# Moving the scatter of two of 36 groups of edge attributes out of the time before graph layer 1, into it

## The chip, the core and the metric

The kernel runs on one core of a Trainium2 chip. The metric is the device time of one launch in microseconds (us). The core has TensorE (matmuls, PE in the profile, PEld for its weight loads), VectorE (DVE), ScalarE (ACT), GpSimd (Pool, POOL in the profile) and SyncE (SP), which here issues DMAs only. Each runs its own program in order; semaphores order them among each other. DMAs are issued by SP, ScalarE and Pool and carried out by 16 DMA engines.

## The reference, cut to what matters

6250 nodes with 128 features, 200000 edges sorted by destination, each with an attribute row of 128 numbers.

```python
# 1. one attention layer on layer-normalised x, added to x
# 2. three graph layers on h = relu(layernorm(x)):
for i in range(3):
    msg = relu(x[src] + edge_attr)                 # 200000 x 128
    aggr = segment_sum(msg, dst, num_segments=6250)
    h = x + aggr
    h = relu(bn(h @ W1[i] + b1[i]))                # bn over all nodes
    x = bn(h @ W2[i] + b2[i])                      # relu after it but for the last
```

All of it is float32. `edge_attr` (102 MB) is read in each of the three layers.

## The kernel before, in words

**Edges and slots.** The edges are cut into 52 and a part groups of 3840 (128 partitions x T = 30 columns). The first 36 groups (`BUCKETS`) are handled in graph layers by source block: there are 49 blocks of 128 source nodes, and each edge of a group gets a slot (rank in its block, block). A table in DRAM, `attr_by_slot` (`attr_table` in the code), has for each group 128 x 49 rows of 128 numbers; an edge's attributes lie at its slot. It is cleared, and then filled by *scatters*: SP loads half a group (15 columns) of attributes into one of two places of `abuf` (`load_half`, L608), and Pool issues an indirect DMA for each column t, which writes 128 rows of 512 bytes to the slots that `ridx[:, g, t]` names (`scatter_half`, L797; the DMA has L808). That makes 36 x 30 = 1080 scatters. The other edges (from 36 x 3840 on) are handled in 69 *units* of 7 x 128 edges, by a gather of the source's row for each column.

**Stages.** Edges are sorted into slots (to about 690 us), with the first 15 half groups scattered beside it. Then comes attention, a loop over 49 blocks x 9 chunks, in which TensorE never rests; Pool scatters the other half groups beside it. A scatter waits at every second column until TensorE's chunks have come to a given point (`s_added`, `PACE`). After attention the rows are normalised and turned, SP stores the node rows and the rows that layer 1 gathers (`gin_rows`), and layer 1 begins. Before its first group VectorE (L1556) and SP (L736) each wait until all scatters have landed; VectorE's wait stands ahead of `rest(0, 0)` (L1566), on which ScalarE's `second_part` (L1050) and, behind it in ScalarE's program, the copies of turned columns (L1030) depend, and with those TensorE's last transposes.

**A graph layer** goes over the 36 groups. A group is 7 chunks of 7 blocks, cut into 14 half steps h (4 and 3 blocks in turn). In each, ScalarE puts attributes into a bank (`seed`, L1074), TensorE adds the source rows by matmuls with one-hot matrices (`gather`, L1910), ScalarE and VectorE take the relu (L1082, L1592), and TensorE adds up by destination (`sum_half`, L1928 and L1931). Once a group, at h = 3, TensorE turns the sum of the group before (L1942). In layer 1 VectorE also makes the one-hot matrix of sources for each chunk (`turn_sources`, L1578), from a row that SP has loaded (L703); SP stores the matrix for the later layers (L698) and loads the attributes of the chunk from the table (L712).

Two units belong to a group, k = 0 and 1. For one, SP loads attributes (`load_unit`, L726), Pool gathers seven times (L853), VectorE adds the two at h = 3 or 10 (`add_unit`, L1612), ScalarE takes the relu (L1094), TensorE sums at h = 6 or 11 (L1952). Pool's program in a layer is a plain row, written out for all 36 groups:

```python
for i in range(BUCKETS):
    for k in [...units of group i...]:
        pool.wait_ge(s_uraw, ...)                  # the unit two before this has been added
        for t in range(tiles_of(i, k)):
            pool.wait_ge(s_used, ... 14 * i + 7 * k + t - GATHER_LEAD)   # half steps summed
            pool.indirect_dma_start(out=unit_x[...], ...)                # L853
```

The gathers may so run up to 10 half steps ahead of the sums. SP's program is a loop over groups, in which the loads of a group are issued beside the work on the group before (`load_group`, L728).

Of the kernel before, what the change touches and what calls it, by code (L numbers as in the profile page):

```python
# [5 lines left out]
ALU = mybir.AluOpType  # L6
ACT = mybir.ActivationFunctionType
AX = mybir.AxisListType
F32 = mybir.dt.float32
# [131 lines left out]
SORT_LOADS = 13  # L141
CLEAR_LOADS = 14
# [15 lines left out]
assert (2 * BUCKETS - SORT_LOADS) * HALF_T // PACE - PACE_AHEAD <= BLOCKS * A_CHUNKS  # L158
# [3 lines left out]
def build(nc, x, src, dst, edge_attr, edge_weight, W, a, W1, b1, g_mlp, be_mlp, W2, b2, g_out, be_out, out):  # L162
    ctx = ExitStack()
    with ctx:
# [101 lines left out]
        row_part = ridx[:, :, :].bitcast(F32)  # L266

# [69 lines left out]
        gsm, at = placed("gsm", [P, 2, STEP], F32, at)  # L337

# [99 lines left out]
        loads = [(g, h * HALF_T, HALF_T) for g in range(BUCKETS) for h in range(2)]  # L438

        def scattered(k):  # L440

            return 16 * sum(n for _, _, n in loads[k % 2:k + 1:2])

# [81 lines left out]
        def _(sp):  # L525
# [202 lines left out]
            def load_group(n, i):  # L728
                before = i - 1 if n == 0 else None
                for h in range(G_HALVES):  # L730
                    if h % 2 == 0:
                        load_chunk(n, i, h // 2, before)
                    if h % BY_UNIT == LOAD_AT and unit_at(i, h) is not None:
                        load_unit(n, i, unit_at(i, h))

# [4 lines left out]
            for n in range(LAYERS):  # L740
                load_group(n, 1)
                with sp.Fori(2, BUCKETS - 1) as i:
                    load_group(n, i)
                load_group(n, BUCKETS - 1)
# [14 lines left out]
        def _(pool):  # L759
# [51 lines left out]

            def listed(t, g, most):
                return pool.value_load(t[0:1, g], min_val=0, max_val=most)
# [21 lines left out]
            for n in range(LAYERS):  # L835
# [8 lines left out]
                for i in range(BUCKETS):  # L844
                    for k in [unit_at(i, h) for h in range(0, G_HALVES, BY_UNIT) if unit_at(i, h) is not None]:
# [3 lines left out]
                        for t in range(tiles_of(i, k)):  # L849

                            half = G_HALVES * i + BY_UNIT * k + t - GATHER_LEAD
                            pool.wait_ge(s_used, G_HALVES * (n * BUCKETS + 1) + half)
                            pool.indirect_dma_start(out=unit_x[:, half_place(k), t, :], out_offset=None, in_=gin_rows[n],  # L853
                                                    in_offset=bass.IndirectOffsetOnAxis(ap=unit_src[:, u, t:t + 1], axis=0)).then_inc(s_ug[half_place(k)], 16)

# [311 lines left out]
        def _(vec):  # L1167
# [148 lines left out]
            def place_rows(g):  # L1316
# [7 lines left out]
                link(vec.scalar_tensor_tensor(ridx[:, g, :], rank[:, g, :], float(BLOCKS), row_part[:, g, :], ALU.mult, ALU.add))  # L1324
                vec.copy_predicated(ridx[:, g, :], left_over[:, g, :].bitcast(I32), trash_row[:, :]).then_inc(s_ridx, 1)
# [704 lines left out]
```

## Time and profile before

| | |
|---|---|
| time, median of 3 runs | 4406.07 us (4400.14 to 4413.49) |
| the profiled execution | 4423.43 us, its span 4421.7 us |
| busy share of the span | PE 89%, DVE 81%, ACT 70%, POOL 70% |
| sorting and first scatters | to about 690 us |
| attention | about 690 to 1832 us |
| layer 1, first to last turn of a group's sum (L1942) | 1974.69 to 2752.09 us |
| scatters (L808) | 1080, 1342.9 us busy |
| gathers of units (L853) | 1449, 1671.4 us busy |

The table is read so: Pool's two kinds of indirect DMA fill (1342.9 + 1671.4) of the 3075.0 us that Pool is busy. The busy time of such a DMA is the time in which Pool makes it, not that in which data moves. The page's shares are averages over stages with different limits, so the rows further down are each of one stretch.

### The profile page before, as it was taken

The numbers are of one execution on the slowest core, as the hardware profiler recorded it, in microseconds if no ns is written. First come the engines' busy times: TensorE is split into PE (matmuls) and PEld (weight loads), VectorE is DVE, ScalarE is ACT, GpSimd is POOL, SyncE is SP. The second block draws the span as 40 slices with busy tenths as digits, with TensorE's granted clock in tenths as the row PEclk, the third lists the DMA queues.
The fourth block names the chain that finished last, engine by engine and source line by source line (L and its number), as shares of the span: only waits on it lengthen the run. The fifth ranks groups of instructions, "written<-read, shape, count | busy, mean of one in ns | idle before, by whom it ended". The sixth has DMA issues, their size and how long they took to land.

```text
span 4421.7 us, 151084 instructions
## 1 busy us (share of the span) xinstructions
PE 3951.3 (89%) x50487; PEld 3786.6 (86%) x50488; DVE 3592.8 (81%) x6829; ACT 3095.0 (70%) x7892; POOL 3075.0 (70%) x2584
## 2 busy tenths in 40 slices
PE   4899966999999999649999999699999979999998
PEld 3899966999999999639999998588898858888896
DVE  7899964777777777538888898699899968899897
ACT  3899954777777777536666676677777767777776
POOL 0388874777777777748787786377777727777773
PEclk7888878999999999869999999799999989999999
DMA  9988878998989889569999998488888838888885
GB/s 141 236 291 269 265 274 263 242 257 244 251 248 252 248 244 254 163 208 328 332 346 328 333 341 291 149 290 295 273 292 288 283 115 273 273 289 293 285 290 171
DMA packets 701344, 1161.55 MB, mean 263 GB/s; under 512 B 155914, under 2 KB 525916, under 8 KB 700908
## 3 DMA queue, kind: packets, MB, share of 16 engines
q1 hardware_dynamic: 486780, 816.61, 55.4%
q10 hardware_dynamic: 133200, 176.14, 16.4%
q0 software_dynamic: 81184, 166.43, 11.3%
q8 instruction: 110, 1.80, 0.2%
q14 instruction: 70, 0.57, 0.0%
HBM read 912.73 MB, written 246.56 MB: 262 GB/s over the span
## 4 chain that ended last, share of the span: by engine, by line
POOL 31%; PE 28%; issue 15%; DVE 11%; DMA 5%; SPq 4%; ACT 3%; DVEq 2%; ACTq 0%; POOLq 0%; PEld 0%; PEldq 0%
POOL attr_by_slot L808 29%; PE ps L1910 10%; PE ps L1928 7%; PE ps L1952 5%; PE ps L1931 3%; DVE dst_hot L1585 3%; DMA unit_x<-gin_rows,unit_src 2%; DVE unit_attr L1612 2%; DVE all_split_msg L1592 2%; POOL unit_x L853 2%; DMA abuf<-in_edge_attr 1%; ACT all_split_msg L1082 1%; PE ps L2003 1%; DVE unit_hot L1608 1%; DVEq L1596 1%
## 5 line engine op out<-in xcount | busy, mean ns | idle before, releaser
L853 POOL DMA_INDIRECT unit_x<-gin_rows,unit_src x1449 | 1671.4, 1153 | 496.2 <-issue 382.0
L808 POOL DMA_INDIRECT attr_by_slot<-abuf,ridx x1080 | 1342.9, 1243 | 505.4 <-issue 327.1
L1910 PE MATMUL ps<-x_parts,src_turned 128*128 128x128 bf16 x15876 | 1153.3, 223 | 99.5 <-ACT ps L1074 69.9
L1910 PEld LDWEIGHTS ps<-x_parts,src_turned 128*128 128x128 fp8e4 x15876 | 955.4, 100 | 164.9 <-issue 122.5
L975 ACT ACTIVATE val<-ps,val 128x128 f32<-128x128 f32 x2597 | 720.0, 376 | 182.9 <-DVE val L1433 182.9
L1074 ACT ACTIVATE ps<-sums 128x512 f32<-128x512 f32 x1512 | 834.9, 552 | 6.0 <-DVE all_split_msg L1592 3.6
L1585 DVE TENSOR_TENSOR dst_hot<-iota_one,dl_slot 128x896 fp32r<-128x896 f32 x756 | 819.9, 1085 | 0.7 <-PE ps L1928 0.7
L1928 PE MATMUL ps<-all_split_msg,dst_hot 128*128 128x256 f32 x3528 | 660.8, 308 | 56.1 <-DVE all_split_msg L1592 47.6
L1592 DVE SCALAR_TENSOR_TENSOR all_split_msg<-ps,all_split_msg 128x512 fp32r<-128x512 f32 x1008 | 607.9, 621 | 110.4 <-ACT all_split_msg L1082 95.3
L1837 PE MATMUL ps<-val,src_hot 128*128 128x129 f32 x5194 | 693.8, 283 | 0.8 <-DVE sums L1373 0.3
L1082 ACT ACTIVATE all_split_msg<-ps 128x512 fp32r<-128x512 f32 x1008 | 546.7, 543 | 143.9 <-PE ps L1910 141.5
L1824 PE MATMUL ps<-h_win,turned_hot 128*128 128x130 bf16 x7791 | 585.6, 221 | 44.3 <-issue 19.8
L1837 PEld LDWEIGHTS ps<-val,src_hot 128*128 128x128 f32 x5194 | 619.7, 192 | 1.3 <-DVE sums L1373 0.5
L1928 PEld LDWEIGHTS ps<-all_split_msg,dst_hot 128*128 128x128 f32 x3528 | 488.6, 194 | 80.0 <-issue 64.3
L1824 PEld LDWEIGHTS ps<-h_win,turned_hot 128*128 128x128 bf16 x7791 | 503.8, 97 | 50.9 <-issue 38.3
L1094 ACT ACTIVATE unit_attr<-unit_attr 128x896 f32<-128x896 f32 x207 | 196.9, 951 | 375.0 <-DVE unit_attr L1612 373.0
L1826 PE MATMUL ps<-s_parts,turned_hot 128*128 (+1 forms) x2597 | 433.2, 167 | 0.0
L1425 DVE TENSOR_TENSOR src_hot<-iota_one,low 128x768 f32<-128x768 f32 (+1 forms) x441 | 415.7, 943 | 0.0
L1952 PE MATMUL ps<-unit_hot,unit_attr 128*128 128x64 f32 x2898 | 355.1, 275 | 16.5 <-ACT unit_attr L1094 16.5
L1952 PEld LDWEIGHTS ps<-unit_hot,unit_attr 128*128 128x128 f32 x2898 | 349.2, 196 | 17.7 <-ACT unit_attr L1094 17.3
L1421 DVE TENSOR_REDUCE z<-ps 128x6 f32<-128x24 f32 (+1 forms) x490 | 83.5, 179 | 272.8 <-PE ps L1826 271.9
L1612 DVE TENSOR_TENSOR unit_attr<-unit_attr,unit_x 128x896 f32<-128x896 f32 x207 | 225.5, 1090 | 76.5 <-DMA unit_x<-gin_rows,unit_src 76.2
(255 smaller groups left out, 5816.2 us busy)
## 6 DMA issues: line engine op xcount, KB each, us to landing
sums<-attr_by_slot SPq DMA_DIRECT2D x756, 448.0 KB
turned_hot<-rows_by_block ACTq DMA_DIRECT2D x392, 384.0 KB
attr_by_slot<-zeros SPq DMA_DIRECT2D x36, 3136.0 KB
unit_attr<-in_edge_attr SPq DMA_DIRECT2D x204, 448.0 KB
abuf<-in_edge_attr SPq DMA_DIRECT2D x72, 960.0 KB
src_row<-rows_by_group SPq DMA_DIRECT2D x252, 224.0 KB
src_turned<-src_hots SPq DMA_DIRECT2D x504, 112.0 KB
src_hots<-src_turned SPq DMA_DIRECT2D x252, 112.0 KB
```

What stands on the lines that cost most here:

```text
L808: pool.indirect_dma_start(out=attr_table, out_offset=bass.IndirectOffsetOnAxis(ap=ridx[:, g, t0 + t:t0 + t + 1], axis=0), in_=abuf[:, k % ...
L853: pool.indirect_dma_start(out=unit_x[:, half_place(k), t, :], out_offset=None, in_=gin_rows[n], in_offset=bass.IndirectOffsetOnAxis(ap=uni ...
L975: ins = act.activation(val[:, slot, t, 0:D], given(slot, t)[:, 0:D], ACT.Copy, scale=val[:, slot, t, D:SUM])
L1074: act.activation(ps[:, BANK[h], 0:tiles * D].rearrange("p (b d) -> p b d", d=D), attr[:, first:first + tiles, :], ACT.Copy).then_inc(s_see ...
L1082: act.activation(to, ps[:, BANK[h], 0:tiles * D].rearrange("p (b d) -> p b d", d=D), ACT.Relu).then_inc(s_msg, 1)
L1585: vec.tensor_tensor(dst_hot[:, HOT[c], :, :], iota_one[:, :].unsqueeze(1).to_broadcast([P, G_TILES, P]), dl.rearrange("p o b -> p (o b)"). ...
L1592: vec.scalar_tensor_tensor(split_msgs[n][:, SPLIT_PLACES[n][c], 1, inner, :], ps[:, BANK[h], 0:tiles * D].rearrange("p (b d) -> p b d", d= ...
L1824: pe.matmul(to[:, 0:ROW], turned_hot[:, 0, at:at + P], window_of(g)[:, part * ROW:(part + 1) * ROW], start=(t % 3 == 0 and part == 0), sto ...
L1837: ins = pe.matmul(ps[:, 6, 0:SUM], src_hot[:, slot, t, :], val[:, slot, t, :], start=(c == 0 and t == 0), stop=(c == A_CHUNKS - 1 and t == ...
L1910: ins = pe.matmul(ps[:, BANK[h], k * D:(k + 1) * D], src_turned[:, b * P:(b + 1) * P], x_parts[:, part, b, :], start=False, stop=(k == til ...
L1928: ins = pe.matmul(ps[:, 7, 0:2 * D].rearrange("p (k d) -> p k d", d=D), dst_hot[:, HOT[c], b % G_TILES, :], split_msgs[n][:, SPLIT_PLACES[ ...
L1952: ins = pe.matmul(ps[:, 6, 0:U_WINDOW], unit_attr[:, half_place(k), t, :], unit_hot[:, half_place(k), t, :], start=(t == 0), stop=(t == ti ...
```

## The change

Groups 34 and 35 (`LATE_GROUPS`) are no longer loaded and scattered by `load_half` and `scatter_half`. Their 60 columns are scattered in layer 1, two in each of the groups 2 to 31, from a buffer of one column, `late_attr`. For r = 0 (group 34) and r = 1 (group 35), SP issues the load of a column in its `load_group` at h = 7 and 13, once the scatter before has landed; Pool issues the scatter behind the gathers of unit k = r, once the load has landed. All semaphores on the scatters ahead of layer 1 now count 34 groups. Ahead of the loads of group 34, SP waits for all late scatters. The slots of the two groups are written to `late_ridx`, at a place that layer 1 doesn't use for anything else. Layers 2 and 3 are not changed.

```diff
+LATE_GROUPS = (BUCKETS - 2, BUCKETS - 1)
+LATE_FROM = 2
+LATE_LOAD_AT = (7, 13)
...
+        late_ridx, _ = placed("late_ridx", [P, 2, T], I32, LATE_AT)
...
+        late_attr, at = placed("late_attr", [P, 1, D], F32, at)
...
-        loads = [(g, h * HALF_T, HALF_T) for g in range(BUCKETS) for h in range(2)]
+        loads = [(g, h * HALF_T, HALF_T) for g in range(LATE_GROUPS[0]) for h in range(2)]
...
+        def late_tile(i, r):
+            return 2 * (i - LATE_FROM) + r
+        LOADED, SCATTERED = len(loads) // 2, len(loads) // 2 * HALF_T
...
+            def load_late(i, r):
+                q, g = late_tile(i, r), LATE_GROUPS[r]
+                sp.wait_ge(s_scat[0], 16 * (SCATTERED + q))
+                of = edge_attr[g * GE:(g + 1) * GE].rearrange("(p t) d -> p t d", t=T)
+                sp.dma_start(late_attr[:, :, :], of[:, bass.ds(i - LATE_FROM, 1), :]).then_inc(s_abuf[0], 16)
...
+            def load_group(n, i, late=False):
                 for h in range(G_HALVES):
                     if h % 2 == 0:
                         load_chunk(n, i, h // 2, before)
                     if h % BY_UNIT == LOAD_AT and unit_at(i, h) is not None:
                         load_unit(n, i, unit_at(i, h))
+                    if late and h in LATE_LOAD_AT:
+                        load_late(i, LATE_LOAD_AT.index(h))
...
+                if n == 0:
+                    with sp.Fori(LATE_FROM, LATE_FROM + T) as i:
+                        load_group(n, i, late=True)
+                    with sp.Fori(LATE_FROM + T, LATE_GROUPS[0]) as i:
+                        load_group(n, i)
+                    sp.wait_ge(s_scat[0], 16 * (SCATTERED + 2 * T))
+                    for i in LATE_GROUPS:
+                        load_group(n, i)
...
+            def scatter_late(i, r):
+                q = late_tile(i, r)
+                pool.wait_ge(s_abuf[0], 16 * (LOADED + q + 1))
+                pool.indirect_dma_start(
+                    out=attr_table, out_offset=bass.IndirectOffsetOnAxis(ap=late_ridx[:, r, i - LATE_FROM:i - LATE_FROM + 1], axis=0),
+                    in_=late_attr[:, 0, :], in_offset=None).then_inc(s_scat[0], 16)
...
                 for k in [...units of group i...]:
                     ...seven gathers...
+                    if n == 0 and LATE_FROM <= i < LATE_FROM + T:
+                        scatter_late(i, k)
...
-                link(vec.scalar_tensor_tensor(ridx[:, g, :], rank[:, g, :], float(BLOCKS), row_part[:, g, :], ALU.mult, ALU.add))
-                vec.copy_predicated(ridx[:, g, :], left_over[:, g, :].bitcast(I32), trash_row[:, :]).then_inc(s_ridx, 1)
+                to = late_ridx[:, LATE_GROUPS.index(g), :] if g in LATE_GROUPS else ridx[:, g, :]
+                link(vec.scalar_tensor_tensor(to, rank[:, g, :], float(BLOCKS), row_part[:, g, :], ALU.mult, ALU.add))
+                vec.copy_predicated(to, left_over[:, g, :].bitcast(I32), trash_row[:, :]).then_inc(s_ridx, 1)
```

## Rows read from the trace of the kernel before

**Rows 1.** Instruction groups on Pool, first 1000 to 1800 us, then 1836 to 1911

```profile
L808 POOL DMA_INDIRECT attr_by_slot<-abuf,ridx x590 | 621.8, 1054 | 179.9 <-issue 179.9
...
L808 POOL DMA_INDIRECT attr_by_slot<-abuf,ridx x59 | 57.9, 982 | 18.0 <-issue 18.0
```

**Rows 2.** Timeline of Pool: start us, us, engine, line [idle before <-releaser]

```profile
1832.80 0.96 POOL L808 DMA_INDIRECT attr_by_slot<-abuf,ridx  x1 [0.30 <-issue]
...
1909.97 0.96 POOL L808 DMA_INDIRECT attr_by_slot<-abuf,ridx  x1 [0.30 <-issue]
```

**Rows 3.** Timeline of DVE and of ACT after attention

```profile
1850.36 0.43 DVE L1548 TENSOR_SCALAR flat<-flat 128x512 f32<-128x512 f32 x1
1912.31 1.09 DVE L1566 TENSOR_TENSOR unit_x<-flat,x_parts 128x896 f32<-128x896 f32 x1 [61.53 <-DMA attr_by_slot<-abuf,ridx]
...
1856.06 1.18 ACT L1030 ACTIVATE agg<-ps 128x512 f32<-128x512 f32 x2 [0.41 <-PE ps L1886]
1913.44 0.95 ACT L1050 ACTIVATE x_parts<-unit_x 128x896 bf16<-128x896 f32 x1 [56.20 <-DVE unit_x L1566]
```

**Rows 4.** Instruction group on Pool in layer 1, 1980 to 2750 us

```profile
L853 POOL DMA_INDIRECT unit_x<-gin_rows,unit_src x483 | 594.8, 1231 | 167.5 <-issue 138.2 <-PE ps L1931 18.0 <-PE ps L1928 11.3
```

**Rows 5.** Waits (us in total, times, longest), layer 1, then layer 2

```profile
DVE unit_attr L1612 <- DMA unit_x<-gin_rows,unit_src: 53.2, 37, 6.4
...
DVE unit_attr L1612 <- DMA unit_x<-gin_rows,unit_src: 9.8, 5, 5.4
```

**Rows 6.** Timeline of PE: the turn at h = 3 of groups 9 to 11

```profile
2154.77 0.61 PE L1942 MATMUL ps<-ident,window_out 128*128 128x128 f32 x4
...
2182.77 0.61 PE L1942 MATMUL ps<-ident,window_out 128*128 128x128 f32 x4
...
2203.25 0.61 PE L1942 MATMUL ps<-ident,window_out 128*128 128x128 f32 x4
```

**Rows 7.** Timeline of Pool: first and last of four long idle times in layer 1

```profile
2155.24 0.94 POOL L853 DMA_INDIRECT unit_x<-gin_rows,unit_src  x1 [5.04 <-PE ps L1931]
...
2689.61 0.94 POOL L853 DMA_INDIRECT unit_x<-gin_rows,unit_src  x1 [4.53 <-PE ps L1931]
```

**Rows 8.** Timeline of DVE and of SP's queue between attention and layer 1

```profile
1840.64 0.19 DVE L1182 TENSOR_SCALAR stat<-ln_mv 128x49 f32<-128x49 f32 x1
...
1875.22 20.66 SPq L530 DMA_DIRECT2D gin_rows<-flat  x13
1919.74 0.37 SPq L703 DMA_DIRECT2D src_row<-rows_by_group  x1
```

**Rows 9.** Timeline of DVE and Pool in layer 1: two that overlap

```profile
2145.87 0.67 DVE L1578 TENSOR_SCALAR src_turned<-src_row,lane_one 128x896 fp8e4<-128x896 bf16 x1
...
2146.08 1.29 POOL L853 DMA_INDIRECT unit_x<-gin_rows,unit_src  x1 [0.30 <-issue]
```

**Rows 10.** Timeline of SP's queue and of DVE in layer 1

```profile
2150.66 0.33 SPq L726 DMA_DIRECT2D unit_attr<-in_edge_attr  x1
...
2153.95 0.33 SPq L703 DMA_DIRECT2D src_row<-rows_by_group  x1
...
2154.23 1.08 DVE L1612 TENSOR_TENSOR unit_attr<-unit_attr,unit_x 128x896 f32<-128x896 f32 x1
```

**Rows 11.** Chain of work in layer 1: start us, us, what

```profile
2100.63 7.52 DMA src_row<-rows_by_group
...
2162.43 6.93 DMA unit_x<-gin_rows,unit_src
```

**Rows 12.** DMA issues of the whole span: count, KB each, median us to landing

```profile
h_win<-att_rows SPq DMA_DIRECT2D x53, 97.5 KB, 2.6
```

**Rows 13.** Stretches of layer 1: us, busy time by engine, PEclk, DMA share, GB/s

```profile
2000.00:2740.00 740.00, 703.33 (x8293) 683.34 (x8290) 645.80 (x966) 501.34 (x1032) 577.38 (x468) 0.98 0.95 335
...
2172.00:2176.00 4.00, 4.00 (x24) 4.00 (x25) 3.55 (x7) 2.29 (x6) 3.12 (x3) 0.50 0.59 216
```

**Rows 14.** Timeline of PE in layer 1, after a long wait

```profile
2171.51 3.25 PE L1952 MATMUL ps<-unit_hot,unit_attr 128*128 128x64 f32 x14 [3.61 <-ACT unit_attr L1094]
```

More of the change, by code:

```diff
@@ L157 @@
 assert ((LOADS_THEN - SORT_LOADS) * HALF_T // PACE - PACE_AHEAD) < LEFT_AT * A_CHUNKS
-assert (2 * BUCKETS - SORT_LOADS) * HALF_T // PACE - PACE_AHEAD <= BLOCKS * A_CHUNKS
+assert LATE_FROM + T <= LATE_GROUPS[0] and BY_UNIT * LATE_FROM >= LATE
+assert (2 * LATE_GROUPS[0] - SORT_LOADS) * HALF_T // PACE - PACE_AHEAD <= BLOCKS * A_CHUNKS
 assert UNITS + LATE == BUCKETS * G_UNITS and G_UNITS == 2 and REST_P == 64 and 1 < REST_U <= U
@@ L266, in build @@
         row_part = ridx[:, :, :].bitcast(F32)
+        LATE_AT = (TOP - 2 * T * 4) // 32 * 32
+        late_ridx, _ = placed("late_ridx", [P, 2, T], I32, LATE_AT)
         fld, at = placed("fld", [P, FIELDS, GROUPS, T], BF16, OVER)
@@ L337, in build @@
         gsm, at = placed("gsm", [P, 2, STEP], F32, at)
+        late_attr, at = placed("late_attr", [P, 1, D], F32, at)
+        assert at <= LATE_AT
         work = sums[:, 0:COLS]
@@ L726, in load_unit @@
                     sp.dma_start(unit_attr[:, half_place(k), :, :].rearrange("p k d -> p (k d)"), of.rearrange("o p e -> (o p) e")).then_inc(s_ua[half_place(k)], 16)
-            def load_group(n, i):
+            def load_late(i, r):
[4 more added lines that the diff above has]
+            def load_group(n, i, late=False):
                 before = i - 1 if n == 0 else None
@@ L741, in _ @@
                 load_group(n, 1)
-                with sp.Fori(2, BUCKETS - 1) as i:
-                    load_group(n, i)
-                load_group(n, BUCKETS - 1)
+                if n == 0:
[6 more added lines that the diff above has]
+                        load_group(n, i)
+                else:
+                    with sp.Fori(2, BUCKETS - 1) as i:
+                        load_group(n, i)
+                    load_group(n, BUCKETS - 1)
                 if n + 1 < LAYERS:
```

## The prediction

> **What bounds the kernel now.** I read the profile in this order: the page's busy shares and costliest groups, the groups of instructions on Pool in three stretches, the timeline around the end of attention, the waits of layers 1 and 2, and single rows of layer 1's timeline.
>
> Between 1000 and 1800 us Pool issues a scatter every (621.8+179.9)/590 = 1.36 us and its idle time is only the 0.30 us that stands ahead of every one [rows 1]. It scatters until 1910 [rows 2], when the rest of the attention layer is long done. There all wait: VectorE has its last normalised rows at 1850.8 and then stands 61.53 us until the scatters have landed, and ScalarE stands 56.20 us behind it [rows 3].
>
> Layer 1 is the second place. Over the stretch that holds all its gathers, 483 of them take 594.8 us busy and 167.5 us idle [rows 4]: (594.8+167.5)/483 = 1.58 us each, of which 483 x 0.30 = 145 us is the fixed lead and only 22 us is more. So Pool has next to no free time there. Is it the bound, or only full? VectorE waits for unit_x 37 times, 53.2 us, in layer 1; in layer 2 only 5 times, 9.8 us [rows 5]. Pool's 14 gathers of a group take 14 x (1.23+0.30) = 21.4 us [rows 4], but a group in which Pool was ahead takes 20.48 us (2182.77 to 2203.25) [rows 6]. So the other engines could do a group in about 20.5 us, and Pool sets 21.4. Layer 1 is bound by Pool by nearly 1 us a group.
>
> Every 112 gathers (8 groups, 128 instructions of Pool with their 16 waits) there is a hole of 4 to 5 us on Pool that no releaser explains: the semaphore named there had passed its mark some 8 us earlier, as the gather asks for half step 124 of the layer and TensorE is in half step 130 [rows 6, 7]. The group around it takes 28.0 us [rows 6]. There are 4 in layer 1, the first at 2155 and the last at 2690 [rows 7].
>
> **The change part by part.**
>
> *Removed ahead of layer 1.* 60 scatters and 4 loads. The last starts at 1909.97 and lands 2.3 us later; the last one that remains, 60 before it, starts at 1832.80 [rows 2], lands by 1836, and is off the path: VectorE needs until 1850.8 for its normalisation, and ScalarE until 1857.2 for its first copies [rows 3]. The attention loop and the pacing of scatters stay: no scatter is moved to an earlier time. ScalarE's wait of 56.20 us goes, since it can start at 1857.2 what it started at 1913.44 [rows 3]. What is late next is SP: it must issue the store of node rows and the 13 stores of layer-1 inputs (20.66 us) before the first load of layer 1 [rows 8]. Before, these lay beside the last scatters. Now they start when the moments are ready (1840.8) and the issuing ends at 1841.3+20.7 = 1862.0; the first load waits also for TensorE's transposes, which ended at 1919.7 and now end at 1919.7-56.2 = 1863.5. So SP is just on time, but the stores' last bytes land some us after their issue, in front of the first loads. Between 0 and 5 us of the 56.2 are lost so; I take 1.2, as issue and transposes meet within 1 us. **Gain 55 us** (51 to 56).
>
> *Added in layer 1: 60 scatters on Pool, two in each of 30 groups.* Pool is the bound there, so this cost isn't hidden. Behind each scatter stand the next unit's seven gathers, and for those VectorE waits. The floor of one is the undisturbed price of the same instruction: 57.9/59+18.0/59 = 1.29 us after attention [rows 1], and its single rows read 0.96+0.30 = 1.26 [rows 2]. The ceiling is the price of a gather in layer 1, 594.8/483+0.30 = 1.53 [rows 4]. The difference is a stretching: a gather beside one of VectorE's L1578 (0.67 us) takes 1.29 instead of 0.94 [rows 7, 9]. VectorE issues the same number of these in a group as before, so I take the stretching of a group as a fixed sum, 14 x (1.23-0.94) = 4.1 us, and what comes on top is the floor: 2 x 1.26 = 2.52 us a group. 30 x 2.52 = **75.6 us** (at the ceiling 30 x 3.06 = 92 us). I take the floor, as the fixed number of VectorE's instructions is the reason for the stretching. The groups get 21.4+2.5 = 24.0 us long.
>
> The Trainium skill (SBUF — State Buffer, section "SBUF: two separate sides") says that VectorE's two-port modes and GpSimd hold one shared port pair exclusively, the loser blocked for the whole instruction, and that descriptors made by GpSimd wait on it. The overlapping rows just named agree. By this rule blocking follows VectorE's instructions, which gives the 75.6; by the plain mean of the rows it would be 92.
>
> *Holes on Pool.* With 18 to 20 instructions of Pool a group for 16 (each scatter with its wait), 128 of them last 6.4 to 7.1 groups for 8: 5 holes for 4. One costs 28.0-21.4 = 6.6 us [rows 6]; I take **5 us** for one more, as part of it falls in slack.
>
> *Added on SP: 60 loads of a tile (64 KB), each behind the landing of the scatter before.* A blocked SP delays the loads of rows and attributes behind it. SP's place for the second late load of a group is behind its second load of a unit, at 2150.66, and the scatter it asks for would land some 1.5 us after the unit's gathers, which VectorE takes at 2154.23 [rows 10]: SP stands 5 us, and the next load of source rows, now at 2153.95, gets 2.5 to 3 us later. It is needed 6 of 14 half steps after VectorE's add: 6 x 24.0/14 = 10.3 us; less 2.5 leaves 7.8 for a load that takes 7.52 [rows 11]. That fits by 0.3 us. Cost: 0 with this margin; if it is gone, VectorE has 24.0-20.5 = 3.5 us a group to hide it in. I take 0.
>
> *The round of the one buffer:* scatter (start to landing, by the gather's row 6.93 us), SP's issue 0.4, load, next scatter. A load lands in 2.6 us (the small window rows of attention) to 7.52 us (source rows in layer 1) [rows 11, 12]. Sum 9.9 to 14.9 us, against 12.0 us for half a group. SP will have issued nothing for some us before each such load, so I take a load at 4 us: 11.3, below 12.0. Bounds 0 and 60 x 2.9 = 174 us. By the Trainium skill (DMA: Bandwidth & Descriptors, section "Anatomy of one DMA — SWDGE (gpsimd) path"), a DMA costs 2.0 us plus its bytes at 436 GB/s, an estimate of 2.2 us for this tile; no trace of layer 1 shows so short a landing (6.93 against it), and by the rule the round would be far from binding.
>
> *Other.* ridx for the two groups goes to another place: nothing. DMA: two loads and two scatters of 64 KB a group beside 7 MB; share 0.95 now [rows 13], and the groups get 12% longer, so it falls. Layers 2 and 3 are as before.
>
> Sum: -55+75.6+5 = **+26 us** (75.6 rests on 30 groups; the remaining 6 keep their time). Profiled execution: 4423.43+26 = 4449. The profiled run lies 17.4 us above the median of the runs, 4406.07; the prediction for the median is **4432 us**.
>
> **The rivals.**
>
> *Layer 1 absorbs the scatters (ends faster).* Place: Pool's row of 14 gathers. Mechanism: the stretching isn't a fixed sum; when VectorE waits more, its fast instructions fall into Pool's 0.30 us leads and Pool wins part of the 4.1 us back. It decides at 55/30 = 1.8 us a group: below it the change gains. With half of the stretching won back a group grows by 2.52-2.05 = 0.5 us: 4406-55+15 = 4366. For it: nothing in the trace shows Pool with 16 DMAs in a group, and layer 2, without the fast instruction, has nearly no such waits [rows 5]. Against: Pool's own pace sets the period, and VectorE waits for it there [rows 5, 6]. Chance 12%.
>
> *The single buffer's round binds, or SP comes late with the source rows.* With a load of 5.5 us the round is 12.8, 0.8 over the half group: +48; with 6.5 us +108. Time 4432+48 = 4480. For it: the two long landings. Against: SP is silent ahead of each such load. Chance 16%.
>
> *TensorE's clock.* Each unit's wait now makes TensorE idle for some 1.8 us twice a group. After a gap of 3.61 us its granted clock is 0.50, that is 1.2 GHz, for 4 us and more [rows 13, 14]. Over the whole of layer 1, with 740-703 = 37 us of idle time mostly in gaps under 1 us, it is 0.98 of 2.4 GHz [rows 13]. 1.8 us lies nearer to the small gaps. If it drops each time, 4 to 6 us at the lower level hold 2 to 3 us less work, and half a group costs TensorE 20.48/2+2 to 3 us, 12.2 to 13.2 for 12.0: +0.2 to +1.2 x 60 = 12 to 72 us; time 4432+40 = 4472. Chance 12%.
>
> *My forecast:* 60%, 4415 to 4448.
>
> **How the numbers follow.** The predicted time is that of the forecast, 4432. What this kernel's runs can tell from no change is about 0.3%, 13 us: faster means below 4393, slower above 4419. Faster: most of the first rival, 10%. Within: the low end of the forecast and the rest of the first rival, 13%. Slower: 77%. The range from 4400 to 4478 leaves out 10% below and 8 to 10% above; it holds the ceiling price of a scatter (4448) and half of the second and third rival. The forecast's own range is 4415 to 4448.
>
> **What would show each step.** Last scatter ahead of layer 1 at 1833; VectorE's first L1566 at about 1852.5, the first src_turned at 1869 to 1872 (before: 4.6 us behind SP's first load, at 1924.3). Groups with late scatters 24.0 us apart, those without (the last ones) 21.4. VectorE's waits for unit_x on nearly every unit, together over 100 us in layer 1. Pool's idle time still 0.30 us ahead of each instruction. If Pool waits for the load of late_attr, the round binds; if TensorE's clock in layer 1 is clearly below 0.98, the third rival. The prediction is wrong if layer 1's groups grow by less than 1.8 us.

## The result, and the profile after

| | before | after |
|---|---|---|
| time, median of 14 runs each | 4408.02 us (4391.31 to 4431.16) | 4386.63 us (4375.36 to 4401.35) |
| ratio after/before, 95% interval | | 0.9955 [0.9943, 0.9967] |
| profiled execution (span) | 4423.43 us (4421.7) | 4388.08 us (4386.4) |

The kernel became 20 us faster (0.45%, by the ratio; 21 by the medians), where 26 us slower was forecast. The direction is wrong, and the time lies under the range.

The stretches of both kernels, cut at the moments after attention (VectorE's TENSOR_SCALAR stat<-ln_mv), at the first unit gather of layer 1 and at the last. Columns: stretch, its length, busy time of each engine with instructions, granted clock, DMA share, GB/s. First before:

```profile
0.00:1840.00 1840.00, 1680.11 (x24857) 1664.84 (x24858) 1438.08 (x3541) 1333.87 (x4334) 1299.85 (x1053) 0.93 0.88 247
1840.00:1979.00 139.00, 48.45 (x422) 42.89 (x423) 49.93 (x90) 51.50 (x101) 70.87 (x65) 0.62 0.49 167
1979.00:2740.00 761.00, 718.06 (x8434) 696.89 (x8430) 657.04 (x985) 511.15 (x1053) 593.65 (x483) 0.97 0.95 334
2740.00:4421.00 1681.00, 1504.72 (x16783) 1382.00 (x16779) 1447.75 (x2216) 1198.47 (x2405) 1110.61 (x985) 0.96 0.76 256
```

and after:

```profile
0.00:1816.00 1816.00, 1681.38 (x24857) 1666.35 (x24858) 1438.70 (x3550) 1334.68 (x4335) 1295.73 (x1048) 0.93 0.88 249
1816.00:1898.00 82.00, 46.58 (x423) 42.42 (x425) 49.23 (x79) 51.23 (x101) 16.80 (x9) 0.75 0.63 216
1898.00:2702.00 804.00, 737.28 (x8430) 711.93 (x8428) 662.18 (x985) 511.04 (x1053) 629.61 (x543) 0.96 0.94 326
2702.00:4386.00 1684.00, 1509.46 (x16782) 1384.99 (x16781) 1447.09 (x2216) 1198.47 (x2405) 1109.80 (x985) 0.95 0.77 255
```

Three things stand there. The front, from the moments to the first gather, went from 139 to 82 us. Layer 1 went from 761 to 804 us. And attention ended 24 us sooner (1816 for 1840), which can't be put down to the change: over the twelve profiled executions from chips like this one, the moments lie at 1820.1 to 1850.0 with all scatters ahead of layer 1, and at 1815.7 to 1839.0 with fewer. So the profiled executions differ by 35 us and the medians by 21, and I compare stretch with stretch. The front and layer 1 give -57+43 = -14 us of the 20; with the 796.6 us that layer 1 takes in a second trace of the kernel after (below) they give -21.

The front after, on Pool, VectorE, SP's queue and ScalarE, to be read beside [rows 2, 3, 8]:

```profile
1811.70 0.96 POOL L840 DMA_INDIRECT attr_by_slot<-abuf,ridx  x1 [0.30 <-issue]
...
1815.70 0.19 DVE L1223 TENSOR_SCALAR stat<-ln_mv 128x49 f32<-128x49 f32 x1
...
1818.62 12.61 SPq L544 DMA_DIRECT2D gin_rows<-flat  x13
...
1827.54 1.09 DVE L1608 TENSOR_TENSOR unit_x<-flat,x_parts 128x896 f32<-128x896 f32 x1 [1.70 <-ACT x_parts L1086]
...
1832.47 0.94 ACT L1091 ACTIVATE x_parts<-unit_x 128x896 bf16<-128x896 f32 x1
...
1837.86 0.36 SPq L717 DMA_DIRECT2D src_row<-rows_by_group  x1
```

The last early scatter starts 4 us ahead of the moments (before: 69 us behind them), and the waits of 61.53 and 56.20 us are gone: VectorE's first L1608 stands 11.8 us behind the moments and ScalarE's first L1091 16.8 us, with 1.70 us and no idle time ahead of them (the forecast had 1852.5 less 1840.8 = 11.7 and 1857.2 less 1840.8 = 16.4). SP's first load of layer 1 stands 22.2 us behind the moments (1837.86 less 1815.70); the forecast had 22.7.

Pool in layer 1 after, all its gathers and late scatters. Columns: count, busy us and mean ns of one, idle us before them and what ended it [rows 4]:

```profile
L892 POOL DMA_INDIRECT unit_x<-gin_rows,unit_src x483 | 563.7, 1167 | 151.7 <-issue 129.7 <-PE ps L1970 13.4 <-PE ps L1973 8.5
L847 POOL DMA_INDIRECT attr_by_slot<-late_attr,late_ridx x60 | 67.1, 1119 | 22.9 <-issue 14.0 <-DMA late_attr<-in_edge_attr 5.5 <-PE ps L1970 3.5
```

This view carries the account of the miss, as Pool's busy and idle time add up to the layer. Before 594.8+167.5 = 762.3 us, after 563.7+151.7+67.1+22.9 = 805.4. The 60 scatters take 90.0 us, but the same 483 gathers take 31.1 us less busy time and 15.8 us less idle time: +43.1.

The waits of layer 1 after (us in total, times, longest), beside [rows 5]:

```profile
DVE unit_attr L1654 <- DMA unit_x<-gin_rows,unit_src: 92.4, 60, 4.5
```

Over the same stretch VectorE waited 38 times, 55.1 us, before; now for 60 of the 68 units that it adds there. The chain of work that ended last, read over the same stretches, has the units' gathers and their transfers in 14% of layer 1 before and in 38% after; in two more traces of kernels with layer 1 as before it has them in 29 and 23%. So layer 1 was Pool's only in part before, and became so for more of its length.

The turn of a group's sum on PE at groups 2 and 32, beside [rows 6]:

```profile
1946.35 0.61 PE L1984 MATMUL ps<-ident,window_out 128*128 128x128 f32 x4
...
2655.14 0.61 PE L1984 MATMUL ps<-ident,window_out 128*128 128x128 f32 x4
```

(2655.14-1946.35)/30 = 23.6 us a group. Before, the same 30 groups took 2025.45 to 2688.45, 22.1 us each: 28.0, 28.4 and 30.2 for the three with a hole (the fourth, 28.8, comes just behind), 20.5 to 22.3 for the others. After, none of them takes over 26.7, and Pool has no idle time over 2.1 us in the layer.

### The profile page after: what moved, and what is told of

The parts are those of the page before. It is cut to its first block, busy times and chain, and to the rows that moved or that the text cites. A ratio compares the mean times of both kernels' runs of the same rounds, so it can differ in the third digit from the quotient of the medians.

```text
span 4386.4 us, 151252 instructions
## 1 busy us (share of the span) xinstructions
PE 3974.7 (91%) x50484; PEld 3805.7 (87%) x50488; DVE 3597.2 (82%) x6829; ACT 3095.4 (71%) x7892; POOL 3051.9 (70%) x2584
## 3 DMA queue, kind: packets, MB, share of 16 engines
q10 hardware_dynamic: 133200, 176.14, 16.4%
q0 software_dynamic: 81184, 166.43, 11.8%
## 4 chain that ended last, share of the span: by engine, by line
PE 57%; DVE 13%; issue 9%; DMA 7%; POOL 5%; ACT 4%; SPq 3%; DVEq 2%; ACTq 0%; POOLq 0%; PEld 0%; PEldq 0%
PE ps L1879 13%; PE ps L1866 11%; PE ps L1952 8%; PE ps L1970 7%; DMA unit_x<-gin_rows,unit_src 5%; PE ps L1994 5%; POOL unit_x L892 4%; DVE unit_attr L1654 3%; DVE dst_hot L1627 3%; PE ps L1807 2%; PE ps L1827 2%; PE ps L1828 2%; DVE all_split_msg L1634 2%; PE ps L1815 2%; PE ps L1973 2%
## 5 line engine op out<-in xcount | busy, mean ns | idle before, releaser
L892 POOL DMA_INDIRECT unit_x<-gin_rows,unit_src x1449 | 1639.2, 1131 | 479.8 <-issue 371.4
L840 POOL DMA_INDIRECT attr_by_slot<-abuf,ridx x1020 | 1284.6, 1259 | 465.6 <-issue 309.0
L1866 PE MATMUL ps<-h_win,turned_hot 128*128 128x130 bf16 x7791 | 583.8, 221 | 26.7 <-ACTq L1019 13.5
```

Of the source, the lines that this page charges most:

```text
L840: pool.indirect_dma_start(out=attr_table, out_offset=bass.IndirectOffsetOnAxis(ap=ridx[:, g, t0 + t:t0 + t + 1], axis=0), in_=abuf[:, k % ...
L1866: pe.matmul(to[:, 0:ROW], turned_hot[:, 0, at:at + P], window_of(g)[:, part * ROW:(part + 1) * ROW], start=(t % 3 == 0 and part == 0), sto ...
```

## The experiments

The measure in all is the stretch of layer 1 from the first unit gather to the last, and the front from the moments to the first. A layer that was traced twice differs by up to 7 us from itself (803.7 and 796.6 in the kernel after), so smaller differences of single traces say nothing. Times are medians with ratios to the kernel before on the same chip. Eight runs fell on chips on which the kernel before itself takes 5120 to 5134 us; they stand by themselves further down, and all else is from chips on which it takes 4408 to 4419.

**The kernel before again.** No edit.

> The kernel before, a second time, for its trace. In the first trace the moments after attention were ready at 1840.6 us and in the trace of the changed kernel at 1815.7, 25 us earlier. Theory A (that differs from execution to execution, the change gives nothing there): here too the moments come at some other point, about as much earlier as the profiled execution is shorter than 4423; the stretch from the moments to the end of layer 1 is 911 us as before. Theory B (the change shortens sorting or attention): the moments come at 1840 again.

4417.06 us, 0.9985 [0.9974, 0.9996]. Front 139.8, layer 1 764.9, four holes 112 gathers apart and 15 gathers over 2.5 us (13 in the first trace). The pattern repeats. The moments come at 1832.5 us, 8 us sooner than in the first trace, so they move without a change. The program is the same, and yet the interval leaves out 1: a ratio 0.15% off 1 is still no difference.

**The front alone.** The kernel after without the late loads and scatters; the attributes of groups 34 and 35 stay at zero in its table.

```diff
-                    if late and h in LATE_LOAD_AT:
-                        load_late(i, LATE_LOAD_AT.index(h))
...
-                        if n == 0 and LATE_FROM <= i < LATE_FROM + T:
-                            scatter_late(i, k)
```

> The changed kernel without its 60 late loads and scatters (the attributes of groups 34 and 35 stay zero): only what is removed ahead of layer 1. Theory A: the gain is ScalarE's wait of 56 us, the time is 4408-56 = 4352, ratio 0.987, and layer 1 has its four holes of 4 to 5 us and groups of 21.4 us as before. Theory B (the removal also shortens sorting or attention by some 25 us): 4408-81 = 4327, ratio 0.982.

4363.04 us, 0.9858 [0.9836, 0.9881], that is 63 us less by the ratio and 56 by the medians (4363.04 for 4418.90). Front 82.0 us and layer 1 759.5 with its four holes and 15 long gathers. The gain of the front is 56 to 58 us (138.5 and 139.8 less 82.0 and 82.4), as the forecast's term of 55 has it, and it leaves layer 1 alone. Over all traces of such chips the front is 135.5 to 141.7 us with every scatter ahead of layer 1 and 81.8 to 82.4 without the last 60.

**The late scatters alone.** The kernel after, but all 36 groups are scattered ahead of layer 1 too; the 60 late loads and scatters write the same rows again.

```diff
-        loads = [(g, h * HALF_T, HALF_T) for g in range(LATE_GROUPS[0]) for h in range(2)]
+        loads = [(g, h * HALF_T, HALF_T) for g in range(BUCKETS) for h in range(2)]
```

> The kernel before, all 36 groups scattered ahead of layer 1, and the 60 late loads and scatters besides (they write groups 34 and 35 a second time). Theory A: layer 1 is 43 us longer, as between the two traces: 60 x 1.42 = 85 us of scatters, less 31 us as gathers are stretched less (1.17 for 1.23 us), less 11 us of idle time: 4451, ratio 1.010. Theory B (my prediction's price, the front having given more): +76 to +81 us, 4486, ratio 1.018.

4467.34 us, 1.0091 [1.0064, 1.0118], +40 us by the ratio and 48 by the medians. Front 141.1, layer 1 798.8: +38 us over the first trace of before and +34 over the one of the same chip, where the forecast's terms give 81. Ahead of its first late scatter Pool waits 4.5 us for the load, its longest idle time in the layer.

**Pool's part without SP's.** As the last, but `late_attr` is loaded once, and SP neither loads nor waits in the groups.

```diff
-                        load_late(i, LATE_LOAD_AT.index(h))
...
-                pool.wait_ge(s_abuf[0], 16 * (LOADED + q + 1))
+                pool.wait_ge(s_abuf[0], 16 * (LOADED + 1))
```

> As the run before, but the buffer is loaded once, so SP issues no late loads and waits for no scatter; Pool issues the same 60 scatters (the first column's attributes go to all slots of the two groups). Theory A1 (Pool's 60 instructions alone set the cost, and what SP does is nothing): +43 us, like e_layer. Theory A2 (SP's blocking spreads the DMA traffic and makes the holes and the stretching smaller): the holes of 4 to 5 us stay, gathers take 1.20 to 1.23 us, and the cost is +60 to +75 us. Theory C (SP's blocking costs): +25 to +35 us.

4461.9 us, 1.0082 [1.0053, 1.0111]. Layer 1 801.6. SP's loads and its waits cost nothing that can be told from the spread of the traces, and neither does the round of the one buffer. Pool's 60 instructions are the cost, and with them alone the long holes are gone: its longest idle time is 1.9 us.

**Gathers for scatters.** As the last, but each of the 60 is a gather into `late_attr` and waits until the one before it has landed.

```diff
-                    out=attr_table, out_offset=bass.IndirectOffsetOnAxis(ap=late_ridx[...], axis=0),
-                    in_=late_attr[:, 0, :], in_offset=None).then_inc(s_scat[0], 16)
+                    out=late_attr[:, 0, :], out_offset=None, in_=gin_rows[0],
+                    in_offset=bass.IndirectOffsetOnAxis(ap=unit_src[:, i, r:r + 1], axis=0)).then_inc(s_scat[0], 16)
```

> 60 further gathers instead of late scatters, all 36 groups scattered ahead. Where before takes 4400 to 4430: theory A (any Pool instruction of this length does it) layer 1 802 us, mean gather 1.15 to 1.18, at most 3 gathers over 2.5 us, no hole over 4 us, ratio 1.008; theory B (it is a matter of scatters) 820 to 845 us, four holes stay, 1.013 to 1.019. Where before takes over 5100: 1.022.

4446.23 us, 1.0091 [1.0074, 1.0107]; layer 1 799.2. Pool's groups in the layer:

```profile
L891 POOL DMA_INDIRECT unit_x<-gin_rows,unit_src x483 | 570.3, 1181 | 148.9 <-issue 121.9 <-PE ps L1973 15.9 <-PE ps L1976 8.0
L846 POOL DMA_INDIRECT late_attr<-gin_rows,unit_src x60 | 63.5, 1058 | 18.3 <-issue 18.3
```

One gather over 2.5 us, one hole of 1.92. So it isn't a matter of scatters: further indirect DMAs of either kind do it, and 43 of the 82 us of these come back.

**Short instructions for DMAs.** The kernel before, with a semaphore increment behind each unit of the groups 2 to 31.

```diff
                             pool.indirect_dma_start(out=unit_x[:, half_place(k), t, :], ...)
+                        if n == 0 and 2 <= i < 32:
+                            pool.sem_inc(s_go, 1)
```

> The kernel before with two semaphore increments a group on Pool in layer 1. Where before takes 4400 to 4430: holes that follow the DMAs stay 112 gathers apart, holes that follow the instructions come nearer (about 105 or less); gathers over 2.5 us anywhere between 0 and 30 if Pool's phase alone decides, layer 1 by it up to 25 us shorter or longer than 761 to 765; if the phase is held by VectorE's waits, 13 to 15 of them again and the same time. Where before takes over 5100: 0.999.

4410.96 us, 1.0008 [0.9993, 1.0023]; layer 1 757.6. The first two of its four holes:

```profile
2132.86 0.94 POOL L853 DMA_INDIRECT unit_x<-gin_rows,unit_src  x1 [5.00 <-PE ps L1933]
...
2309.65 0.96 POOL L853 DMA_INDIRECT unit_x<-gin_rows,unit_src  x1 [4.97 <-PE ps L1933]
```

They stand ahead of the 114th, 226th, 338th and 450th gather of the layer, as before. So the forecast's count by instructions ("128 of them last 6.4 to 7.1 groups") was wrong: 60 more instructions move no hole. There are 13 long gathers again, each begun 0.05 to 0.06 us ahead of VectorE's add. Delays of this size on Pool don't move the gathers against VectorE.

**A part of the dose: 45 and 31 late scatters.** In the first version group 34's first half is scattered ahead of layer 1; its second half comes behind the first unit of groups 2 to 16, and group 35 behind the second unit as in the kernel after. In the second, 14 of those 15 columns are loaded into `unit_attr`, which is free until layer 1's units need it, and scattered between Pool's seven third parts of x, where Pool idles.

```diff
-                        if n == 0 and LATE_FROM <= i < LATE_FROM + T:
+                        if n == 0 and LATE_FROM <= i < LATE_FROM + (HALF_T if k == 0 else T):    # 45; with 31: 1 if k == 0
...
+        pro_attr = unit_attr[:, :, :, :].rearrange("p a k d -> p (a k) d")
...
                     pool.tensor_tensor(x_parts[:, 2, of, :], unit_x[:, c % 2, :, :], x_parts[:, 1, of, :], ALU.subtract)...
+                    if n == 0:
+                        for t in range(sum(PRO_AFTER[:c]), sum(PRO_AFTER[:c + 1])):   # PRO_AFTER = (0, 4, 1, 3, 1, 2, 3)
+                            pool.wait_ge(s_abuf[1], 16 * (len(loads) // 2 + 1))
+                            pool.indirect_dma_start(out=attr_table, ...late_ridx[:, 0, HALF_T + 1 + t:...],
+                                in_=pro_attr[:, t, :], in_offset=None).then_inc(s_scat[1], 16)
```

> The version with 45 late columns. Where the kernel before takes 4400 to 4430: theory A (0.7 us net a late scatter, in proportion) layer 1 from the first gather to the last 793 us, ratio 0.9935; theory B (what comes back needs two scatters a group) 802 us, ratio 0.996. Where before takes over 5100: 1.011, as in the two looks so far.

> The version with 31 late columns and 14 in the front. Where before takes 4400 to 4430: theory A layer 1 782 us, front 2 to 6 us longer than with 60 late ones, ratio 0.991; theory B 804 us and 0.996. Where before takes over 5100: 1.001.

> The version with 31 late columns and 14 in the front, for its time beside the kernel after. Where before takes 4400 to 4430: layer 1 783 us, first gather at moments + 86, so 17 us (804 less 783, less 4 of the front) under the kernel after: ratio to before 0.992. If what it saves in layer 1 comes back elsewhere (the front's third parts of x, or the attention stage), it is 0.995 as the kernel after. Where before takes over 5100: 1.001.

> The kernel after beside it on the same chip. Where before takes 4400 to 4430: 0.9955. Where before takes over 5100: 1.017, its layer 1 909 us.

| late scatters | layer 1, us | front, us | time, us | ratio [95%] |
|---|---|---|---|---|
| 45 | 793.0 | 85.2 | 4387.98 | 0.9958 [0.9941, 0.9974] |
| 31, beside 45 | 782.8 | 86.4 | 4380.10 | 0.9932 [0.9908, 0.9957] |
| 31, beside after | 776.5 | 86.6 | 4383.90 | 0.9927 [0.9908, 0.9945] |
| 60 (after), on that chip | 796.6 | 81.8 | 4397.03 | 0.9957 [0.9942, 0.9971] |

Without late scatters layer 1 is 757.6 to 764.9 in four traces, mean 760.7. So 31 cost 19 us (0.61 each), 45 cost 32 (0.72), 60 cost 36 to 43 in five traces (one of them with gathers for scatters), mean 39 (0.66). What comes back does not need two scatters a group; that rival theory, with 804 us for 31, falls. But the parts that it comes back in are not in proportion. Pool's groups with 31, in the trace beside after:

```profile
L914 POOL DMA_INDIRECT unit_x<-gin_rows,unit_src x483 | 581.2, 1203 | 147.6 <-issue 129.5 <-PE ps L1996 13.5 <-PE ps L1999 4.6
L863 POOL DMA_INDIRECT attr_by_slot<-late_attr,late_ridx x31 | 39.2, 1265 | 10.0 <-issue 8.8 <-DMA late_attr<-in_edge_attr 0.9 <-PE ps L1996 0.3
```

Idle time is 19.9 us down, all that the holes held (no idle time over 0.9 us), while the gathers won back only 13.6 us, 13 of them being over 2.5 us as before. One more DMA a group (and 14 in the front) is enough against the holes, but the long gathers go only where VectorE waits. In the traces of 0, 31, 45 and 60 late scatters VectorE waits for 38, 43, 42 and 60 of 68 units, and 13, 13, 12 and 2 gathers are long; with 31 beside 45 it was 31 and 23, and in the second trace of after 65 and 1.

The holes did not go without a trace. In all six traces with 45 or 60 further DMAs Pool still stands 1.7 to 2.7 us ahead of the 114th DMA of the layer, counted with the further ones; without them that place has the first hole, of 4.3 to 5.0 us. The next short ones, with 60 scatters and their loads, stand ahead of the 224th and the 432nd, so the count of 112 holds no longer. And in layers 2 and 3, which the change leaves alone, the kernel after has four holes each of 4.1 to 5.1 us, 112 gathers apart.

The version with 31 beats the kernel before by 31 us, and where it ran beside the kernel after its median is 13 us under that (4383.90 for 4397.03). Against after that is not certain: the two intervals just touch. The one with 45 has 7 us less in layer 1 than the mean of those with 60 (800.0) and 3 us more in the front; its time can't be told from after's.

**The same on chips where before takes 5120 to 5134 us.** There were two such chips: the versions of 45 and 31, the kernel after and the 60 gathers ran on one, and the versions and after again with the short instructions on the other, with the same ratios expected or those of the first.

> 45 columns late instead of 60: group 34's first half is scattered ahead as before, its second half behind the first unit of groups 2 to 16, group 35 behind the second unit of groups 2 to 31. Theory A (each late scatter costs its 1.42 us and brings back about 0.7 us of shorter gathers and smaller holes, in proportion): layer 1 from the first gather to the last 793 us (760 without, 803 with 60), front 2 us longer than with 60 late ones, time 8 to 9 us under the kernel after, ratio to the kernel before 0.9935. Theory B (what comes back needs two scatters a group): the 15 groups with one scatter pay its full 1.42 us and the holes of 4 to 5 us are back in them; layer 1 about 802 us, time as the kernel after or 2 us over it, ratio 0.996.

> 31 columns late: as the version of 45, but 14 of the 15 columns of group 34's second half are loaded into the buffer of the units' attributes, which is free until its first load at 76 us behind the moments, and scattered between Pool's seven third parts of x ahead of the first gather (4, 1, 3, 1, 2 and 3 behind the second to the seventh), in its idle time of 6 to 14 us between them. Theory A (0.7 us a late scatter): layer 1 from the first gather to the last 782 us; the front 2 us longer, and up to 4 more where a third part now waits for a scatter that has begun: 15 to 21 us under the kernel after, ratio 0.991. Theory B (one scatter a group brings nothing back, 31 x 1.42 = 44): 804 us, time as the kernel after or over it, ratio 0.996. If the scatters in the front hold up the third parts by a whole scatter each (7 x 1.26 = 9 us), the first gather stands at moments + 93 instead of + 84.

> The kernel after again, beside the two versions on the same chip: ratio to the kernel before 0.9955 within its interval of 0.994 to 0.997; layer 1 from the first gather to the last 800 to 805 us, no hole over 2.5 us in it.

> All 36 groups scattered ahead as in the kernel before, and behind each unit of groups 2 to 31 one more gather (the rows of gin that the unit's first or second column names, into the one-tile buffer), 60 in all, each waiting for the one before it. Nothing is stored in DRAM by them. Theory A (any further Pool instruction of this length gives the gathers another phase to VectorE, and takes away the long gathers and the holes): layer 1 802 us, mean of the units' gathers 1.15 to 1.18, gathers over 2.5 us at most 3, no hole over 4 us, ratio 1.008 as with the 60 scatters. Theory B (what matters is that they are scatters, whose stores leave the reads' queue free): full price 60 x 1.42 = 85, less the 26 us of the long gathers at the most, the four holes stay: layer 1 820 to 845 us, ratio 1.013 to 1.019.

> The kernel before with one short instruction more on Pool, a semaphore increment, behind each of the two units of groups 2 to 31 in layer 1 (60 in all, no transfer, nothing left out). Pool runs 14 gathers and 2 waits, now and 2 increments, a group. Theory A (a hole of 4 to 5 us falls every so many DMAs of Pool's queue, 112 in layer 1): the four holes stay 112 gathers apart. Theory B (every so many instructions fetched): they come at a smaller distance, about 105 gathers. Both: the time changes by less than 3 us, layer 1 760 us, the mean gather 1.23. If what the late scatters brought back is a matter of Pool's phase alone, a delay of some 0.1 us twice a group changes the number of gathers over 2.5 us from 13 to something else between 0 and 30, and layer 1 with it by up to 25 us.

| | ratio on the first | on the second | layer 1, us |
|---|---|---|---|
| short instructions | | 0.9994 [0.9965, 1.0023] | 819.8 |
| 31 late | 1.0011 [0.9980, 1.0043] | 1.0014 [0.9989, 1.0040] | 845.3 |
| 45 late | 1.0106 [1.0042, 1.0169] | 1.0115 [1.0071, 1.0159] | 879.7 |
| after, 60 late | 1.0173 [1.0114, 1.0232] | 1.0176 [1.0124, 1.0228] | 909.4 |
| 60 gathers | 1.0221 [1.0138, 1.0305] | | 899.0 |

The last column is of the second chip's traces, for the 60 gathers of the first's, where the kernel after has 915.8. Here the change makes the kernel slower. The stretches of the kernel with the short instructions (it stands for before, 0.9994), cut 3 us ahead of the moments:

```profile
0.00:2310.00 2310.00, 1849.26 (x24857) 1753.59 (x24858) 1432.00 (x3505) 1320.88 (x4334) 1275.32 (x1108) 0.88 0.74 199
2310.00:2395.00 85.00, 46.74 (x421) 42.53 (x423) 52.42 (x126) 51.28 (x101) 17.15 (x9) 0.74 0.64 209
2395.00:3215.00 820.00, 744.65 (x8420) 699.90 (x8418) 666.60 (x983) 509.00 (x1050) 591.25 (x483) 0.97 0.91 310
```

and two of its rows, Pool's last scatter and the moments:

```profile
2282.84 0.95 POOL L808 DMA_INDIRECT attr_by_slot<-abuf,ridx  x1 [0.94 <-remote]
...
2313.04 0.19 DVE L1184 TENSOR_SCALAR stat<-ln_mv 128x49 f32<-128x49 f32 x1
```

The time up to the moments is 470 us longer, with 199 GB/s moved for 247, and the last scatter starts 30 us ahead of the moments. So there is no wait in front of layer 1 to remove: the front is 82 us with all 36 groups scattered ahead (2313.0 to 2395.2) and 83 in the kernel after. The front gains nothing, and layer 1 costs 909.4-819.8 = 90 us. The medians differ by 76 (5197.18 for 5121.61), and in the two traces of after the moments come at 2261.7 and 2262.6 us, 50 sooner than here. Whether fewer scatters beside attention shorten it on such a chip no run shows: on the other kind of chip the moments move by 34 us from trace to trace. Pool's gathers in layer 1, first with the short instructions, then after:

```profile
L853 POOL DMA_INDIRECT unit_x<-gin_rows,unit_src x483 | 592.2, 1226 | 228.9 <-issue 114.9 <-PE ps L1930 63.7 <-PE ps L1933 28.5
```

```profile
L892 POOL DMA_INDIRECT unit_x<-gin_rows,unit_src x483 | 577.5, 1196 | 226.4 <-issue 108.2 <-remote 47.7 <-PE ps L1970 45.7
L847 POOL DMA_INDIRECT attr_by_slot<-late_attr,late_ridx x60 | 74.8, 1247 | 32.4 <-DMA late_attr<-in_edge_attr 15.6 <-issue 13.2 <-PE ps L1970 1.9
```

The layer is not Pool's there: its gathers have 229 us of idle time for 168, VectorE waits for a unit only 3 times, and no gather is over 2.5 us from the start. The four holes are there too, 4.6 to 5.1 us, and in the kernel after no idle time is over 2.8 us. Yet the idle time does not shrink by the scatters (226), the gathers give back 15 us, and the full 107 us of the scatters come on top but for that. The gathers for scatters, with no load by SP, cost 79 us over the short instructions of the other chip and are 17 us under after on their own; so most of it is Pool's further DMA again. Why a Pool with free time passes the price on is open, as is what makes these chips slower. One rival that no run took apart is TensorE's clock: over the layer it is 0.97 with the short instructions and 0.94 after, and TensorE is busy 781 us for 745 with the same matmuls.

## Why the prediction was wrong

**Gain ahead of layer 1, 55 us.** Right: 56 to 58, with nothing lost to SP's stores. Its reason is also confirmed by the chips on which it isn't there: where the scatters end ahead of the moments, the front is 82 us with or without the change.

**60 scatters at 1.26 us, 75.6 us.** Under the mark but between its ends: 90.0 us by Pool's group (1.12 busy and 0.38 idle each), 5.5 of it waits for the load. The floor rested on the next step, and without any load the 60 still take 66.6+18.3 = 84.9 us.

**The stretching of a group as a fixed sum.** This step failed: I held that it stays with VectorE's number of instructions, so nothing comes back. The gathers gave back 31.1 us, (1.231-1.167) x 483. What I priced as 14 x (1.23-0.94) spread evenly was in large part 13 single gathers. One of them, Pool and VectorE before:

```profile
2012.99 2.96 POOL L853 DMA_INDIRECT unit_x<-gin_rows,unit_src  x1 [0.30 <-issue]
...
2012.51 0.63 DVE L1608 TENSOR_TENSOR unit_hot<-iota_one,unit_dl 128x448 f32<-128x448 f32 x1
2013.05 1.09 DVE L1612 TENSOR_TENSOR unit_attr<-unit_attr,unit_x 128x896 f32<-128x896 f32 x1
2014.05 1.09 DVE L1585 TENSOR_TENSOR dst_hot<-iota_one,dl_slot 128x896 fp32r<-128x896 f32 x1
2015.05 0.69 DVE L1578 TENSOR_SCALAR src_turned<-src_row,lane_one 128x896 fp8e4<-128x896 bf16 x1
2015.65 1.35 DVE L1592 SCALAR_TENSOR_TENSOR two_split_msg<-ps,two_split_msg 128x512 fp32r<-128x512 f32 x2
```

VectorE did not wait for the unit, so its instructions stand back to back, and Pool's gather, begun 0.06 us ahead of the add (L1612), lasts until 0.21 us behind L1578, the third from the add on. It is over while L1592, which has one of its inputs in PSUM, still runs. Each of the 13 looks so. With 60 late scatters VectorE waits, the row is broken up, and two are left: 11 x 2.0 = 22 of the 31 us. That it is these instructions that hold the gather was read from the rows and not tried by taking one away. The Trainium skill (SBUF — State Buffer, section "A bandwidth-pool intuition that's wrong (but worth ruling out)") has a Pool DMA beside one `tensor_copy` of VectorE blocked until VectorE's end plus some 115 ns; here the end is at +0.21 us, behind three instructions. The Trainium skill (SBUF — State Buffer, section "Who interferes with whom") lets TENSOR_TENSOR with both inputs in SBUF hold up GpSimd's reads, but infers that it doesn't stop the making of descriptors; in this row an undisturbed gather of 0.94 us would have been over at 2013.93, within the TENSOR_TENSOR that began behind it, so by this reading one of them held it. Whether it is the gather's reading of its row numbers that was held no run shows.

**Holes on Pool, +5 us for a fifth.** This step failed too. There are four before and none over 2.1 us after. The fault is 37.5 us (80.6 forecast, 43.1 measured), and it can be split in two ways. In Pool's own account the scatters cost 14.4 more than forecast (90.0 for 75.6), the gathers gave back 31.1 for nothing, and idle time fell by 15.8 where I had added 5, which is 20.8. In groups: those without a hole grew from 21.4 to 23.6 us, 2.2 for the 2.5 of the forecast, which is 66 us in 30 groups; four groups with a hole gave back 26 us, at the forecast's own price of 6.6 each, where I had added 5. By this account 31 are the holes, and it comes to 40 us and leaves 3 over. That the 2.2 lies so near to the 2.5 is luck: dearer scatters and shorter gathers made up for each other. I extrapolated a pattern whose cause I didn't know, by a count of instructions that the run with short instructions shows to be no cause. The holes shrink or go with 31 further DMAs in the layer. Why, is open.

**SP and the round of the one buffer, 0.** Right: with SP's part taken out layer 1 is 801.6 for 798.8, no more apart than two traces of one kernel.

**The rivals.** The one that came nearest is "layer 1 absorbs the scatters", in its place (Pool's row of gathers) and its turning point, 1.8 us a group: the layer grew by 43.1/30 = 1.4. I gave it 12%, with the argument that Pool's pace sets the period. It set it only in part: VectorE waited for 38 of 68 units, and the layer held 23 us of idle time beyond the leads and 13 x 2.0 = 26 us of long gathers, of which more work on Pool took most away. What the rival named as its means, VectorE's fast instructions falling into Pool's leads, isn't shown. TensorE's clock is not ruled out as a part of the 43 us: it is 0.96 for 0.97 over the layer, and TensorE is busy 737 us for 718 with the same matmuls. The signs named for the forecast (groups of 24.0 us, VectorE waiting on nearly every unit, over 100 us) came out nearly as named, at 23.6 us and 60 of 68 units with 92 us; they could not tell forecast from result, since I had compared 24.0 with the 21.4 of a group without a hole and not with the mean of 22.1.

## What to carry to other kernels

Before work is priced onto a busy engine by the sum of its instructions, ask of each part of its time whether it belongs to the instruction or to the phase that it stands in: compare the distribution, not the mean (13 of 483 gathers held 26 us), and never continue a periodic stall by a count whose cause no run has shown. A wait that is removed is worth what it is in this regime only: where another stage gets slower, it isn't there, while the work that was moved keeps its price. And if work leaves a full stretch, look first for idle time on the same engine: 14 scatters in the gaps of the front cost some 1.3 us there (86.5 for 85.2) and saved 10 to 17 in the layer (782.8 and 776.5 for 793.0).

## What the runs showed of the hardware that was not expected

- An indirect DMA of 128 rows on Pool takes 0.94 to 0.96 us (gather or scatter) and 0.30 us ahead of it when nothing disturbs it, and 2.96 us beside a run of back-to-back VectorE instructions; it ends about 0.21 us behind the third from its start on.
- With 14 such DMAs a group Pool stands 4.3 to 5.6 us in layer 1 after every 112, ahead of the 114th, 226th, 338th and 450th, for no releaser that the profile shows. 60 semaphore increments among them don't move that; 31 more DMAs (and 14 in the front) take it away, and 45 or 60 leave 1.7 to 2.7 us at the first place.
- The same program took 4408 to 4419 us on some chips and 5120 to 5134 on two others, with 199 GB/s for 247 up to the end of attention, and the verdict on the change turned with it (0.9955 and 1.0176).
